# Decoder block with cross attention: more context tiles as three rounded products, shifts moved to VectorE, a shorter score ring and straight code

## The reference

```python
x = _layernorm(x + self_attention(x))                    # 16 heads of 16, causal
# cross attention: 16 heads of 128, 1500 keys of width 128 per image
q = rmsnorm((x @ Wq).reshape(B, Sq, H, D), gq)
k = rmsnorm((ctx @ Wk).reshape(B, Skv, H, D), gk)
v = (ctx @ Wv).reshape(B, Skv, H, D)
attn = softmax(einsum('bqhd,bkhd->bhqk', q, k) / sqrt(D))
x = _layernorm(x + einsum('bhqk,bkhd->bqhd', attn, v).reshape(B, Sq, H * D) @ Wo)
x = _layernorm(x + gelu(x @ proj1.T + b1) @ proj2.T + b2)
```

## Time and profile before

| | before |
|---|---|
| runs (us) | 1346.9, 1342.68, 1343.91; median 1343.91 |
| profiled execution (us) | 1344.18, span 1342.4, clock 0.996 |
| busy: PE, PEld | 1308.3 (97%), 1032.9 (77%) |
| busy: DVE, ACT, POOL | 1109.5 (83%), 1022.0 (76%), 1042.1 (78%) |
| chain that ended last | PE 83% of the span |

### The profile page before, as it was taken

How to read it: one execution, slowest core, us unless ns; L and a number is a source line. 1 busy time by engine, 2 the same in 40 slices (tenths; PEclk the granted TensorE clock), 3 DMA queues, 4 the chain that set the end, 5 groups by cost and what they waited for, 6 DMA issues and landing times.

```text
span 1342.4 us, 25133 instructions
## 1 busy us (share of the span) xinstructions
PE 1308.3 (97%) x6366; PEld 1032.9 (77%) x6366; DVE 1109.5 (83%) x1745; ACT 1022.0 (76%) x3155; POOL 1042.1 (78%) x937
## 2 busy tenths in 40 slices
PE   8789899999999999999999999999999999999998
PEld 4667578777777777777777777777777777778787
DVE  4867589888888888888888888888888888886675
ACT  2666688888888888888888888888888888873442
POOL 3843252899898889888988898889888989898850
PEclk9999899999999999999999999999999999999999
DMA  7040230101010101010101010101010101030210
GB/s 250 33 168 1 69 144 9 39 9 39 9 39 9 40 8 39 8 40 8 39 8 40 8 39 8 40 8 39 8 40 8 39 8 39 1 110 1 79 57 28
DMA packets 29181, 53.99 MB, mean 40 GB/s; under 512 B 2864, under 2 KB 23984, under 8 KB 27264
## 3 DMA queue, kind: packets, MB, share of 16 engines
q1 hardware_dynamic: 28336, 52.64, 11.6%
q10 hardware_dynamic: 720, 0.10, 0.0%
HBM read 44.60 MB, written 8.13 MB: 39 GB/s over the span
## 4 chain that ended last, share of the span: by engine, by line
PE 83%; DVE 3%; DMA 1%; issue 1%; ACT 0%; DVEq 0%; ACTq 0%
PE xa_k_ps L1331 13%; PE xa_k_ps L1332 13%; PE xa_k_ps L1333 13%; PE xa_o_ps L1416 12%; PE xa_s_ps L1333 5%; PE xa_s_ps L1331 5%; PE xa_s_ps L1332 5%; PE om_ps L1422 3%; PE xa_o_ps L1331 2%; PE xa_o_ps L1332 2%; PE xa_o_ps L1333 2%; DVE xa_ss L1263 1%; PE xa_o_ps L1348 1%; PE xa_o_ps L1356 1%; PE om_ps L1682 1%; PE om_ps L1683 1%
## 5 line engine op out<-in xcount | busy, mean ns | idle before, releaser
L1331 PE MATMUL xa_k_ps<-wk_parts,xa_ctxT_hi 128*125 128x512 f32 x768 | 376.9, 491 | 6.0 <-DVE wk_parts L1323 4.9
L1263 DVE TENSOR_REDUCE xa_ss<-xa_sq 125x6 f32<-125x768 f32 x360 | 339.3, 942 | 1.1 <-ACT xa_sq L1192 1.1
L1251 DVE TENSOR_TENSOR xa_scores<-xa_s_ps,xa_rk 125x448 f32<-125x448 f32 x384 | 238.2, 620 | 98.0 <-PE xa_s_ps L1333 96.2
L1332 PE MATMUL xa_k_ps<-wk_parts,xa_ctxT_hi 128*125 128x512 f32 x768 | 303.8, 396 | 0.0
L1333 PE MATMUL xa_k_ps<-wk_parts,ctxT_lo 128*125 128x512 f32 x768 | 303.0, 395 | 0.0
L1103 POOL TENSOR_TENSOR xa_den<-probs,xa_den 125x896 f32<-125x896 f32 x128 | 272.7, 2130 | 3.5 <-ACT probs L1177 3.5
L1177 ACT ACTIVATE probs<-xa_scores 125x896 f32<-125x896 f32 x192 | 183.6, 956 | 100.9 <-DVE xa_scores L1291 38.2
L1157 ACT ACTIVATE xa_sq<-xa_k_ps 125x512 f32<-125x512 f32 x360 | 212.5, 590 | 40.8 <-PE xa_k_ps L1333 21.7
L1191 ACT ACTIVATE xa_k_ps<-xa_k_ps 125x128 f32<-125x128 f32 x720 | 189.2, 263 | 30.4 <-PE xa_k_ps L1333 28.3
L1416 PE MATMUL xa_o_ps<-probs,xa_ctx_nat 125*128 125x448 f32 x448 | 205.4, 539 | 0.0
L1271 DVE TENSOR_TENSOR xa_max_ps<-xa_scores,xa_max_ps 125x448 f32<-125x448 f32 x320 | 198.1, 619 | 0.6
(11 more groups left out here) (184 smaller groups left out, 2353.6 us busy)
## 6 DMA issues: line engine op xcount, KB each, us to landing
xa_ctx_nat<-in_ctx SPq DMA_DIRECT2D x16, 750.0 KB
ctxT_in<-in_ctxT SPq DMA_DIRECT2D x84, 125.0 KB, 2.0
qo<-in_xq_w SPq DMA_DIRECT2D x1, 2048.0 KB, 11.8
qo<-in_xo_w SPq DMA_DIRECT2D x1, 2048.0 KB, 18.9
vo_scratch<-qo SPq DMA_DIRECT2D x2, 1024.0 KB, 4.9
w_parts_scratch<-ws_hi SPq DMA_DIRECT2D x2, 1024.0 KB, 4.2
w_parts_scratch<-ws_lo SPq DMA_DIRECT2D x2, 1024.0 KB, 5.9
vo<-vo_scratch SPq DMA_DIRECT2D x1, 2048.0 KB, 9.8
```

The lines of the kernel that those rows point to most:

```text
L1251: dve.tensor_tensor(scores[0:KP, j, :, :], raw, key_scale, ALU.mult).then_inc(s_taken, 1)
L1263: dve.tensor_reduce(ss[:, i // 2, UH * (i % 2):UH * (i % 2) + vector_heads(of)], squares(of, i).rearrange("p (g d) -> p g d", d=XD), AX.X, ...
L1331: pe.matmul(out, l_hi, r_hi, start=first, stop=False)
L1332: pe.matmul(out, l_hi, r_lo, start=False, stop=False)
```

## The change

Tiles 2, 8 and 10 of each half join the odd ones: 8 of 12 tiles are now summed as three rounded products (`PAIR_SPLITS` counts the split tiles of each pair). For pairs 1, 4 and 5 ScalarE therefore makes `p_hi` of both tiles (896 columns instead of 448), and GpSimd the rest of both. The heads of the context are kept once instead of twice and are made in three pieces late in the image (steps 17, 17 and 21, their rests at 18, 18 and 23) instead of two (steps 8 and 12, rests at 9 and 13), and TensorE waits for each piece at its first tile. The shift of the pair 6 goes from GpSimd (t=8) to VectorE (t=7), so that VectorE has four of six; the semaphore `shift_done` that linked the two engines becomes one for each. The score ring has 20 places, taken by a running count. The loop is gone: all phases are straight code on every engine. Not shown below: the offsets of overlaid tiles, and one semaphore in place of two in the storing of the MLP's weights.

```diff
-def each_phase(eng, body, loop_end):
-
-    for b in (-1, 0, 1):
-        body(Phase(b))
-    with eng.Fori(1, loop_end // 2) as pair:
-        for i in range(2):
-            body(Phase(None, pair, i))
-    for b in range(loop_end, B + 1):
+def each_phase(body):
+
+    for b in range(-1, B + 1):
         body(Phase(b))
...
 ADDS = KT // 2
 PV_LAG = EXP_LAG + 5
 LOW_LAG = EXP_LAG + 3
-NAT_SPLITS = (8, 12)
 TD = 8
 TD_LAST = 6
 NPR = 8
...
+VECTOR_SHIFTS = {2: 0, 4: 2, 6: 4, 7: 6}
+VS, GS = 4, 2
+
+
 def vector_shifts(y):
 
-    return y % KT < KT // 2
-
-
+    return y % KT < 2 * VS
+
+
+def vector_shifts_done(ph, y):
+
+    last = ph.b + y // STEPS == B - 1 and y // KT % 2
+    return ph.at(2 * VS, VS * (y // KT) + (y % KT // 2 + 1 if last else min(y % KT // 2 + 1, VS)))
+
+
+def pool_shifts_done(ph, y):
+    return ph.at(2 * GS, GS * (y // KT) + y % KT // 2 + 1 - VS)
+
+
+PAIR_SPLITS = (0, 2, 1, 1, 2, 2)
+SPLIT_TILES = [2 * i + o for i, n in enumerate(PAIR_SPLITS) for o in range(2 - n, 2)]
+NAT_PARTS = ((2, 4), (5, 6), (7, 12))
+NAT_HI_AT = {17: (0, 1), 21: (2,)}
+NAT_LO_AT = {18: (0, 1), 23: (2,)}
+SC = 20
 SPLIT_PAIRS = KT // 2 - 1
 
 
 def pairs_split(ph, y):
 
     return ph.at(2 * SPLIT_PAIRS, SPLIT_PAIRS * (y // KT) + y % KT // 2)
-
-
...
-        nat_hi = sb("xa_nat_hi", [KP, 2, SPLIT_PAIRS, C], F32R)
-        p_hi = sb("xa_p_hi", [KP, NPR // 2, UW], F32R)
+        nat_hi = sb("xa_nat_hi", [KP, len(SPLIT_TILES), C], F32R)
+        p_hi = sb("xa_p_hi", [KP, NPR // 2, 2, UW], F32R)
         q_hi = sb("xa_q_hi", [P, 2, UH, T], F32R)
         q_lo = sb("xa_q_lo", [P, 2, UH, T], F32R)
-        scores = sb("xa_scores", [P, STEPS, UH, T])
+        scores = sb("xa_scores", [P, SC, UH, T])
...
+        def score_slot(ph, j):
+            return scores[0:KP, ph.at(STEPS, j) % SC, :, :].rearrange("p h q -> p (h q)")
+
+        def score_pair(ph, y):
+            slot = ph.at(STEPS, y) % SC
+            return scores[0:KP, slot:slot + 2, :, :].rearrange("p s h q -> p s (h q)")
...
+        def nat_part(nat, ph, part):
+            return nat[:, ph.parity(), slice(*NAT_PARTS[part]), :]
+
+        def nat_hi_part(part):
+            first, last = NAT_PARTS[part]
+            at = SPLIT_TILES.index(first)
+            return nat_hi[:, at:at + last - first, :]
...
-                        if y % KT == KT // 2:
+                        if y % KT == 2 * VS:
                             pool.wait_ge(gmax_ready, ph.at(2, y // KT + 1))
-                        pool.wait_ge(shift_done, ph.at(STEPS, y))
-                        pool.tensor_tensor(score_pair(y), score_pair(y), gmax_pair(y), ALU.subtract
-                                           ).then_inc(shift_done, 2)
+                            pool.wait_ge(max_done, ph.at(2 * (KT - 1), (KT - 1) * (y // KT + 1)))
+                        pool.tensor_tensor(score_pair(ph, y), score_pair(ph, y), gmax_pair(y), ALU.subtract
+                                           ).then_inc(pool_shifted, 1)
...
-                        pool.tensor_tensor(probs_r[0:KP, (y + 1) % NPR, :], probs[0:KP, (y + 1) % NPR, :],
-                                           p_hi[:, y // 2 % (NPR // 2), :].bitcast(F32), ALU.subtract
+                        first = 2 - PAIR_SPLITS[y % KT // 2]
+                        slots = slice(y % NPR + first, y % NPR + 2)
+                        pool.tensor_tensor(probs_r[0:KP, slots, :], probs[0:KP, slots, :],
+                                           p_hi[:, y // 2 % (NPR // 2), first:2, :].bitcast(F32), ALU.subtract
                                            ).then_inc(p_lo_ready, 1)
-                    if j - 1 in NAT_SPLITS and ph.within(0, 15):
-                        part = NAT_SPLITS.index(j - 1)
-                        pool.wait_ge(nat_hi_ready, ph.at(2, part + 1))
-                        pool.tensor_tensor(odd_tiles(nat_r, ph, part), odd_tiles(ctx_nat, ph, part),
-                                           odd_hi(ph, part).bitcast(F32), ALU.subtract).then_inc(nat_lo_ready, 1)
+                    if ph.within(0, 15):
+                        for part in NAT_LO_AT.get(j, ()):
+                            pool.wait_ge(nat_hi_ready, ph.at(len(NAT_PARTS), part + 1))
+                            pool.tensor_tensor(nat_part(nat_r, ph, part), nat_part(ctx_nat, ph, part),
+                                               nat_hi_part(part).bitcast(F32), ALU.subtract).then_inc(nat_lo_ready, 1)
...
-                        wait(act, shift_done, ph.at(STEPS, KT * (h - 2)))
-                        act.activation(gmax[:, 1 - h, :], o_ps[0:KP, 1 - h, 0:UW], ACT.Copy
-                                       ).then_inc(gmax_ready, 1)
+                        wait(act, pool_shifted, ph.at(2 * GS, GS * (h - 2)))
+                        act.activation(gmax[:, 1 - h, :], o_ps[0:KP, 1 - h, 0:UW], ACT.Copy).then_inc(gmax_ready, 1)
...
-                        wait(act, shift_done, ph.at(STEPS, y + 2))
+                        if vector_shifts(y) or ph.b == B and y >= -KT:
+                            act.wait_ge(vector_shifted, vector_shifts_done(ph, y))
+                        else:
+                            act.wait_ge(pool_shifted, pool_shifts_done(ph, y))
                         wait(act, pv_done, ph.at(STEPS, y - NPR + 2))
                         if ph.b is None or STEPS * ph.b + y >= NPR:
                             wait(act, den_done, adds_done(ph, y - NPR))
-                        act.activation(probs_pair(y), score_pair(y), ACT.Exp).then_inc(exp_done, 2)
-                        if y % KT:
-                            act.activation(p_hi[:, y // 2 % (NPR // 2), :], score_slot(y + 1), ACT.Exp
+                        act.activation(probs_pair(y), score_pair(ph, y), ACT.Exp).then_inc(exp_done, 2)
+                        if PAIR_SPLITS[y % KT // 2] == 2:
+                            act.activation(p_hi[:, y // 2 % (NPR // 2), :, :], score_pair(ph, y), ACT.Exp
                                            ).then_inc(p_hi_ready, 1)
-                    if j in NAT_SPLITS and ph.within(0, 15):
-                        part = NAT_SPLITS.index(j)
-                        act.wait_ge(nat_loaded[ph.parity()], nat_loads(ph))
-                        act.activation(odd_hi(ph, part), odd_tiles(ctx_nat, ph, part), ACT.Copy).then_inc(nat_hi_ready, 1)
+                        elif y % KT:
+                            act.activation(p_hi[:, y // 2 % (NPR // 2), 1, :], score_slot(ph, y + 1), ACT.Exp
+                                           ).then_inc(p_hi_ready, 1)
+                    if ph.within(0, 15):
+                        for part in NAT_HI_AT.get(j, ()):
+                            act.wait_ge(nat_loaded[ph.parity()], nat_loads(ph))
+                            wait(act, pv_done, ph.at(STEPS, NAT_PARTS[part][1] - KT))
+                            act.activation(nat_hi_part(part), nat_part(ctx_nat, ph, part), ACT.Copy).then_inc(nat_hi_ready, 1)
                     if ph.within(-1, 14):
...
-                        wait(dve, exp_done, ph.at(STEPS, j - STEPS + 1))
-                        dve.tensor_tensor(scores[0:KP, j, :, :], raw, key_scale, ALU.mult).then_inc(s_taken, 1)
+                        wait(dve, exp_done, ph.at(STEPS, j - SC + 1))
+                        dve.tensor_tensor(scores[0:KP, ph.at(STEPS, j) % SC, :, :], raw, key_scale, ALU.mult
+                                          ).then_inc(s_taken, 1)
...
-                    y = lagged_pair(ph, j, SHIFT_LAG)
-                    pairs = [y] if y is not None and vector_shifts(y) else []
+                    pairs = [KT * (h - 1) + VECTOR_SHIFTS[t]] if t in VECTOR_SHIFTS and ended_half(ph, h) else []
                     if ph.b == B:
                         pairs = list(LAST_SHIFTS.get(j, ()))
                     for y in pairs:
                         if y % KT == 0:
                             dve.wait_ge(gmax_ready, ph.at(2, y // KT + 1))
-                        wait(dve, shift_done, ph.at(STEPS, y))
-                        dve.tensor_tensor(score_pair(y), score_pair(y), spread_pair(y), ALU.subtract
-                                          ).then_inc(shift_done, 2)
+                        dve.tensor_tensor(score_pair(ph, y), score_pair(ph, y), spread_pair(y), ALU.subtract
+                                          ).then_inc(vector_shifted, 1)
                     for b, step, tile in EARLY_STATS:
                         if ph.b == b and j == step:
...
                         if ty == 0:
-                            pe.wait_ge(shift_done, ph.at(STEPS, y + (KT if ph.b == B else KT // 2)))
+                            pe.wait_ge(vector_shifted, vector_shifts_done(ph, y + KT - 2))
                             pe.wait_ge(gmax_ready, ph.at(2, y // KT + 1))
                             wait(pe, o_taken, ph.at(2, y // KT - 1))
                             if hy == 0:
                                 pe.wait_ge(nat_loaded[of.parity()], nat_loads(of))
```

(41 more changed lines are left out.)

19 lines of the change are left out of this document (7 added, 12 removed).

## The result

| | before | after |
|---|---|---|
| median of 8 runs each, same chip (us) | 1345.0 | 1347.7 |
| lowest to highest (us) | 1342.68 to 1346.9 | 1346.14 to 1348.92 |
| profiled span (us) | 1342.4 | 1345.1 |

The account below looks back on a forecast made before the run. TensorE's queue was taken to set the pace. Against the profiled 1344.18 us, -13.6 + 4.2 + 1.2 + 3.0 + 2.1 = -3.1 gave 1341.1, or 1340.8 for the median; range 1332 to 1350.

Parts of the forecast that it names:

- The gain on TensorE: Weighted sums of tiles 2, 8 and 10: 96 sums, each 0.142 us shorter as three rounded products, 13.6 us less.
- What is added to the helpers: Added work per half: GpSimd 1.3 us, ScalarE some 1.4, VectorE one shift of 1.08; no engine passes TensorE in the sum.
- Chain 1: GpSimd over an image's middle: its last rest comes late for P(10), the sum of tile 10; 0.3 us, 14 times, +4.2.
- Chain 2: VectorE's shifts up to P(0), the sum of tile 0: wait of 0.03 us a half, taken as 0.
- Image 0: VectorE is saturated there, so the moved shift of pair 6 delays P(0): 1.2 us, once (0.5 to 1.5).
- Chain 3: The end: P(8) in image 15 waits for GpSimd's rest, 3.0 us (1.5 to 4); last half's P(10), 2.1 (0 to 3).
- The rest at nothing: Ring of 20, single context heads, split semaphores, straight code for the loop and SyncE's transfers: no cost or gain.
- The likeliest case: The forecast itself: the whole kernel 3.1 us faster, 1340.8 for the median (1336 to 1346), chance 0.46.
- rival A: GpSimd is in time in the middle, so no wait of P(10) there: -8.4 us, 1335.5 (1331 to 1338), chance 0.24.
- C: Rival: P(0) waits for VectorE's shift of pair 6 by 0.25 us in each half: +8, 1348.8, chance 0.06.
- the sum of both upper bounds, 7: Upper bounds of the two waits forecast at the end: 4 us for image 15's P(8), 3 for the last half's P(10).

Follow-up runs that it names:

- run 2: The changed kernel with ScalarE's two context heads of step 17 moved to steps 14 and 16: 1341.1 us, ratio 0.9974.
- Run 7: The changed kernel with useless products on TensorE filling the waits before two late sums, tile 8 in image 15's phase and tile 10 in the last: 1345.7 us, ratio 1.0004.
- runs 1: The kernel before with only its loop over images 1 to 13 written out as straight code: 1343.8 us, ratio 0.9996.
- run 9: The changed kernel with tiles 2, 8 and 10 of all images as fp32 sums, the rest of the change kept: 1346.7 us, ratio 1.0010.
- run 5: The changed kernel with context heads at steps 14, 16 and 21 and tiles 8 and 10 of images 14 and 15 as fp32 sums: 1332.1 us, ratio 0.9910.
- run 8: As run 5, plus image 0's six changed sums as fp32 and its first half's pair 6 shift on GpSimd: 1331.1 us, ratio 0.9907.

## Why the prediction was wrong, step by step

**The gain on TensorE** was right: 0.143 us a sum measured against 0.142. The estimate by the four passes of the Trainium skill's page "FP8 and Floating Point Precision" (section "TensorE Precision Notes"), 0.19 us a sum and 18 us in all, is not borne out.

**What is added to the helpers** was right: 2.13, 0.94 and 1.57 us for the three new shapes.

**Chain 1** was right in its own sum and wrong in what it met. Counted from the turned maximum of the same half (626.89 us before, 626.55 after), `den_lo` starts at 17.14 instead of 16.60, 0.5 us later (forecast 0.7); from there to the end of GpSimd's last rest are 30.9 us (forecast 30.75); the rest ends at 48.03, where the forecast has 48.06. But P(10) stands at 48.39 and not at the forecast's 47.94, because TensorE had already waited for P(0), and so nothing is left to wait for. The step that failed is the one on ScalarE's two heads, priced at 0.5 us. It followed them to `den_hi` and to TensorE's K place, and wrote "nothing is added". It left out their third reader, VectorE's reduce. In run 2, with the heads moved, `den_lo` starts at 16.65 and the rest ends at 47.56, in time as well: the late heads delay both chains, and the first wait hides most of the second (an estimate from these rows: 48.03 + 0.16 against 48.39 - 0.41 leaves 0.2 us).

**Chain 2** failed for the same reason. It moved VectorE's rows rigidly by 0.14 us and found 0.03 us of wait. Those rows have no wait for squares in them; after, the reduce waits 0.39 us for them. All VectorE work up to the shift follows, and P(0) comes some 0.4 us late in each of the 13 h=1 halves of the middle: (902.88 - 897.61) / 13 = 0.41 us. The forecast's 4.2 us for chain 1 and 0 for chain 2 are 0 and 5.3. That the price of the two is so near is luck.

**Image 0** was sized 1.2 and cost 2.06 + 0.14 = 2.2 us. The wait of P(0) was right, 1.16 us. Another one was missed: TensorE waits 1.9 us for ScalarE's squares in that half, against 1.0 before. Run 2, which moves the heads, has 1.3 there and gives 0.5 us back.

**Chain 3** had the first wait right in place and cause: P(8) of image 14, in image 15's phase, waits 3.43 us for GpSimd's rest, and this half costs 3.36 + 0.43 = 3.8 us (forecast 3.0). The second wait is not where the forecast put it. It named the P(10) of the last half, at 1289.4. The one that waits 2.16 us is the P(10) of the half before it, 21 us earlier, which was priced at nothing; the last P(10) shows no idle time in front (TensorE, then GpSimd, after):

```profile
1268.95 0.47 PE L1349 MATMUL xa_o_ps<-xa_p_hi,xa_nat_hi 125*128 125x448 f32 x1 [2.16 <-POOL probs_r L1129]
...
1290.15 0.71 PE L1349 MATMUL xa_o_ps<-xa_p_hi,xa_nat_hi 125*128 125x448 f32 x1
...
1240.72 1.16 POOL L1135 TENSOR_TENSOR xa_nat_r<-xa_ctx_nat,xa_nat_hi 125x256 fp32r<-125x256 f32 x2 [6.54 <-ACT xa_nat_hi L1204]
...
1287.68 2.14 POOL L1129 TENSOR_TENSOR probs_r<-probs,xa_p_hi 125x896 fp32r<-125x896 f32 x1
```

and the stop that GpSimd had there before:

```profile
1272.67 2.09 POOL L1103 TENSOR_TENSOR xa_den<-probs,xa_den 125x896 f32<-125x896 f32 x1 [3.54 <-ACT probs L1177]
```

So 2.2 us measured against 2.1 forecast is luck. The step added 2 x 0.97 us to GpSimd's last rest alone. In the trace GpSimd's stop of 3.54 us is gone, it works with no gap above 0.2 us from 1240.72 to 1289.82, and its last rest ends 31.61 us behind the last turned maximum instead of 28.41, 3.2 us later. The last stretch costs 3.36 + 5 x 0.143 = 4.1 us against 2.1. With 0.45 us for the wait of P(0) in image 14 and 0.4 that no row explains, the end costs 6.67 + 14 x 0.143 = 8.7 us against 5.1.

The step also priced a wait at its length. Run 7 shows what that leaves out: after standing idle, TensorE ran for a time at its lower clock level, and 1.9 us of the end in the trace (2.7 in the medians) go with it. In the last half the two can't be parted cleanly, since GpSimd's pace holds TensorE there in run 7 as well: the last P(10) waits 0.62 us for its rest.

**The rest at nothing** was right for ring, single heads and straight code in the middle images (runs 1 and 9).

**The rivals.** The changed kernel follows none of them. The likeliest case and rival A were both right that the middle gains; C named the wait that came, but for a shift that is too much in each half, and run 9 shows that by itself it is not. The range, 1332 to 1350, held the time. In chances the weight was on the wrong side: the end's 8.7 us lie above the sum of both upper bounds, 7.

**The gain was there to be had**: with heads at 14, 16 and 21 and the last two images' tiles 8 and 10 left alone, the same change is 0.90% faster than the kernel before (run 5), 12 us by the ratio. With image 0 mended too it is 0.93% (run 8), which the intervals don't tell from run 5.
